# A decoder on one core: first norm's root moved to VectorE, GELUs, result banks and context masks re-ordered

## What is computed

```python
x = layernorm(x + L0_attn(x))              # 16 heads, Student-t kernel on rotated q, k
x = layernorm(x + L0_xattn(x, ctx, ctx))   # mLSTM cell: input and forget gates, 8 heads
x = layernorm(x + L0_ffn(x))               # shared MLP + 8 experts, top 2, GELU
x = layernorm(x + L1_attn(x)); x = layernorm(x + L1_xattn(x, ctx)); x = layernorm(x + L1_ffn(x))

def layernorm(x): return (x - mean(x)) / sqrt(var(x) + 1e-5)

# mLSTM gates
ig, fg = concat(q, k, v) @ igate_w.T + igate_b, concat(q, k, v) @ fgate_w.T + fgate_b
cs = cumsum(log_sigmoid(fg)); log_D = cs[s] - cs[t] + ig[t]; m = max_t(log_D)
# expert e on its tokens: gelu(x @ w1[e] + b1[e]) @ w2[e] + b2[e]
```

## Time and profile before

| what | value |
|---|---|
| median of 3 runs | 2462.15 us (2458.47 to 2462.42) |
| the profiled execution | 2459.75 us |
| its span, first to last instruction | 2457.9 us |
| mean granted TensorE clock | 0.904 of full speed |
| TensorE matmul busy | 1925.9 us (78%) |
| VectorE busy | 1672.9 us (68%) |
| ScalarE busy | 1113.1 us (45%) |
| GpSimd busy | 842.4 us (34%) |
| chain that ended last | TensorE 38%, VectorE 36%, issue 11%, ScalarE 6%, GpSimd 6%, DMA 3% |

### The profile page before, as it was taken

The page is one execution under the profiler, slowest core; times in us unless marked ns, Lnnn a source line. Parts: engine busy times, 40 slices in busy tenths (PEclk is TensorE's granted clock), DMA queues, the critical chain, the costliest instruction groups (busy, mean ns, idle before and its releaser), DMA issues.

```text
span 2457.9 us, 39681 instructions
## 1 busy us (share of the span) xinstructions
PE 1925.9 (78%) x14136; PEld 1375.3 (56%) x14136; DVE 1672.9 (68%) x3985; ACT 1113.1 (45%) x3168; POOL 842.4 (34%) x775
## 2 busy tenths in 40 slices
PE   2786698778886898788886788689877888675698
PEld 1465356645675456645674467545664567553355
DVE  8895794669737893669656993779566973713355
ACT  2462266335642565336642564246533564232234
POOL 0562363226512562317421661236322651211000
PEclk8997799889997999889997999799988999787799
DMA  4000011202030012201030103101120104051000
GB/s 137 1 1 9 13 57 52 77 10 70 1 119 19 16 55 73 64 10 61 6 122 11 56 15 103 34 14 57 50 79 10 69 1 119 9 208 56 9 13 22
DMA packets 72746, 117.08 MB, mean 48 GB/s; under 512 B 7822, under 2 KB 46870, under 8 KB 72038
## 3 DMA queue, kind: packets, MB, share of 16 engines
q1 hardware_dynamic: 67014, 101.42, 12.9%
q0 software_dynamic: 5536, 13.12, 1.8%
HBM read 95.18 MB, written 18.81 MB: 46 GB/s over the span
## 4 chain that ended last, share of the span: by engine, by line
PE 38%; DVE 36%; issue 11%; ACT 6%; POOL 6%; DMA 3%; SPq 1%; DVEq 0%; POOLq 0%; ACTq 0%
PE bank L1355 35%; DVE work L495 11%; DVE bank L504 5%; DVE work L513 3%; DVE work L493 3%; ACT work L952 3%; DVE max L794 2%; POOL hid L1263 2%; PE bank L1359 2%; POOL work L1243 1%; ACT act_row L952 1%; DMA hid<-y_sorted,slot_id 1%; POOL work L1238 1%; DVE acc L712 1%; DMA w_ring<-in_w_routed 1%
## 5 line engine op out<-in xcount | busy, mean ns | idle before, releaser
L1355 PEld LDWEIGHTS bank<-work 128*128 128x128 f32 (+2 forms) x5152 | 387.8, 200 | 182.7 <-issue 181.5
L1355 PE MATMUL bank<-work 128*128 128x128 f32 (+2 forms) x5152 | 418.8, 307 | 69.2 <-DVE max L794 42.2
L952 ACT ACTIVATE work<-bank 128x512 f32<-128x512 f32 (+1 forms) x560 | 247.0, 516 | 311.9 <-PE bank L1355 256.6
L495 DVE TENSOR_TENSOR work<-bank,table_space 64x512 f32<-64x512 f32 x512 | 352.2, 688 | 6.8
L1231 POOL TENSOR_TENSOR work<-work 128x512 f32<-128x512 f32 x128 | 163.3, 1276 | 350.5 <-DVE work L495 248.7
L952 ACT ACTIVATE work<-work 128x512 f32<-128x512 f32 (+1 forms) x338 | 196.7, 618 | 169.8 <-DVE work L581 73.4
L952 ACT ACTIVATE work<-work,negmax 128x128 f32<-128x128 f32 x512 | 199.0, 390 | 100.2 <-DVE negmax L515 100.2
L1238 POOL TENSOR_TENSOR work<-sb_ident,nrm 128x512 f32<-128x512 f32 x128 | 133.1, 1039 | 274.4 <-ACT nrm L952 274.4
L1355 PE MATMUL bank<-work,table_space 128*128 128x512 f32 x256 | 141.3, 634 | 89.9 <-DVE negmax L515 59.4
L952 ACT ACTIVATE hid<-bank,w_ring 128x128 f32<-128x128 f32 x480 | 136.5, 370 | 160.0 <-PE bank L1355 159.9
L493 DVE TENSOR_TENSOR work<-bank,table_space 128x512 f32<-128x512 f32 x256 | 173.8, 679 | 32.4 <-POOL work L1243 20.0
(11 more groups left out here) (287 smaller groups left out, 3414.8 us busy)
## 6 DMA issues: line engine op xcount, KB each, us to landing
w_ring<-in_w_routed SPq DMA_DIRECT2D x120, 514.0 KB, 4.3
x_quad<-x_sorted SPq DMA_DIRECT2D x24, 256.0 KB, 2.9
y_sorted<-y_quad SPq DMA_DIRECT2D x24, 256.0 KB, 2.7
x_T<-in_x_T POOLq DMA_DIRECT2D x9, 256.0 KB, 3.1
x_row<-in_x_row POOLq DMA_DIRECT2D x9, 256.0 KB, 3.9
ctx_T<-in_ctx_T SPq DMA_DIRECT2D x8, 256.0 KB, 2.6
work<-in_ctx_row SPq DMA_DIRECT2D x8, 256.0 KB, 3.0
out<-act_row SPq DMA_DIRECT2D x8, 256.0 KB, 2.3
```

The source lines that it names most:

```text
L495: last = v.tensor_tensor(rows(wk[i + 1][o]), rows(src[p]), sinT[o, s].unsqueeze(1).broadcast_to([DH0, GB, N]), ALU.mult)
L952: return nc.scalar.activation(o, i, f, **k)
L1355: return nc.tensor.matmul(o, l, r, start=start, stop=stop, skip_group_check=True)
```

## The change

1. Norm: the first norm's 1/sqrt is no longer made by ScalarE. VectorE makes it itself (`inverse_root`): half the variance, a starting value from the bits, three Newton steps, 11 instructions on `[128, 4]`. It stands between the copies of blocks 2 and 3.
2. GELUs: those of units 7 and 8 run before the gates' Exp and Ln, so the table is changed behind unit 8 and not behind unit 6. TensorE's transpose of `row_x`, the gates' matmul and the two gate transposes move behind units 7, 8, 10 and 14 (before: 6, 7, 9 and 11).
3. VectorE's gate steps are cut into more pieces and spread between the copies.
4. Banks: the down results of blocks 4, 6, 8, ... go to bank 7, the others to bank 6; a down waits for the copy of the block two before it, and block 4 for `attn_out`.
5. Masks: GpSimd starts the masked contexts behind `gate_max` and not behind `attn_out`.

The diff:

```diff
--- before.py
+++ after.py
@@ -144,6 +144,7 @@
         norm_x, norm_t = Norm("norm_x"), Norm("norm_t")
         centre, centred = sb("centre", 128, GB), sem("centred")
 
+        half_var, root = sb("half_var", 128, GB), sb("root", 128, GB)
         nrm = sb("nrm", 128, 2, 8)
         norm_rows = sb("norm_rows", 128, 2, N)
         negmax = sb("negmax", 128, 2, GB)
@@ -230,6 +231,10 @@
 
             return min(GB, BLOCKS - GB * q)
 
+        def y_bank(i):
+
+            return 7 if i > 3 and i % 2 == 0 else 6
+
         def prob_T_bank(h):
 
             return 6 if h < H0 - 5 else (h - (H0 - 5)) % 2
@@ -453,6 +458,19 @@
 
                 norm_stats(n, src)
                 norm_apply(n, g, i, src, dst, per, ahead)
+
+            def inverse_root(n):
+
+                half, y, y2 = half_var[:], n.rstd[:], root[:]
+                link(v.tensor_scalar(half, n.mv[:, :, 1], 0.5, 0.5e-5, ALU.mult, ALU.add))
+                link(v.tensor_scalar(y.bitcast(i32), half.bitcast(i32), -0.5, 1593268703.0, ALU.mult, ALU.add))
+                for step in range(3):
+                    link(v.tensor_tensor(y2, y, y, ALU.mult))
+                    link(v.scalar_tensor_tensor(y2, y2, -1.0, half, ALU.mult, ALU.mult))
+                    last = v.scalar_tensor_tensor(y, y2, 1.5, y, ALU.add, ALU.mult)
+                    if step < 2:
+                        link(last)
+                last.then_inc(n.ready, 1)
 
             def bc(m):
 
@@ -551,6 +569,8 @@
                     c = slice(b * N, b * N + N)
                     last = v.tensor_tensor_scan(m_g[:, c], one_row, a_g[:, c], -3.0e38, ALU.mult, ALU.max)
                 link(last)
+
+            def gates_parts(g, d):
 
                 link(v.tensor_copy(m_parts[0:8, :], m_g[:]))
                 link(v.tensor_tensor(logf[:], m_g[:], m_parts[0:8, :], ALU.subtract))
@@ -701,7 +721,7 @@
                 q = i // GB
                 if q >= 2 and i % GB == 0:
                     dve.wait_ge(y_stored[q % 2], g * (LOAD // 2 * 16) + q // 2 * 16)
-                v.tensor_copy(y_quad[q % 2][:, i % GB], rows(bank[6])[:, i % GB]).then_inc(y_out, 1)
+                v.tensor_copy(y_quad[q % 2][:, i % GB], rows(bank[y_bank(i)])[:, i % GB]).then_inc(y_out, 1)
 
             def combine(g):
 
@@ -741,6 +761,10 @@
                     norm_stats(norm_x, resid_a)
                 if experts:
                     take_block(2, g)
+                if heads:
+                    dve.wait_ge(norm_x.stats, tally(g, d, LNS, 1))
+                    inverse_root(norm_x)
+                if experts:
                     take_block(3, g)
                 if heads:
                     norm_apply(norm_x, g, 0, resid_a, row_x, ahead=d)
@@ -748,20 +772,28 @@
                     take_block(4, g)
                 if heads:
                     gates_forget(g, d)
-                    gates_scan(g, d)
                 if experts:
                     take_block(5, g)
                     take_rows(2, g)
                     take_block(6, g)
                 if heads:
+                    gates_scan(g, d)
+                if experts:
+                    take_block(7, g)
+                if heads:
                     gates_max(g, d)
+                if experts:
+                    take_block(8, g)
+                if heads:
+                    gates_parts(g, d)
+                if experts:
+                    take_block(9, g)
+                    take_rows(3, g)
+                    take_block(10, g)
+                if heads:
                     gates_columns(g, d)
                 if experts:
-                    take_block(7, g)
-                    take_block(8, g)
-                    take_block(9, g)
-                    take_rows(3, g)
-                    for i in range(10, BLOCKS):
+                    for i in range(11, BLOCKS):
                         take_block(i, g)
 
             def experts_norm(g):
@@ -1046,9 +1078,8 @@
                 for n in range(SLOTS):
                     fn(k2[n], bank[1][:], ACT.Copy, scale=slot_mask[:, n:n + 1]).then_inc(k2_masked, 1)
 
-            def attn0_norm(g, d):
-
-                norm(norm_x, g, 0, ahead=d)
+            def attn0_T(g, d):
+
                 act.wait_ge(stored, tally(g, d, 32, -16) if d else 16)
                 act.wait_ge(x_tr, tally(g, d, 2, 1))
                 fn(seq_T[:], bank[1][:], ACT.Copy).then_inc(x_T_sb, 1)
@@ -1113,12 +1144,17 @@
                         attn0_slot(s, g, d)
                     if experts:
                         for j in IN_SLOT[s - DRAIN]:
-                            gelus(j, g, heads and j == 6)
+                            gelus(j, g)
+                if experts:
+                    gelus(7, g)
                 if heads:
-                    attn0_norm(g, d)
+                    attn0_T(g, d)
+                if experts:
+                    gelus(8, g, heads)
+                if heads:
                     gates_forget(g, d)
                 if experts:
-                    for j in range(7, UNITS):
+                    for j in range(9, UNITS):
                         gelus(j, g, j == UNITS - 1)
                 if heads:
                     gates_total(g, d)
@@ -1266,7 +1302,7 @@
             def xattn(g, d):
 
                 pool.wait_ge(in_ctx, tally(g, d, 32, 32))
-                pool.wait_ge(attn_out, tally(g, d, 1, 1))
+                pool.wait_ge(gate_max, tally(g, d, 1, 1))
                 for h in range(H1):
                     if d and 2 <= h < 4:
                         pool.wait_ge(quad_tr, g * LOAD + h + 1)
@@ -1481,11 +1517,13 @@
                 i = j - 2
                 if i == 0:
                     pe.wait_ge(moe_acc, g + 1)
+                elif i == 4 and heads:
+                    pe.wait_ge(attn_out, tally(g, d, 1, 1))
                 else:
-                    pe.wait_ge(y_out, g * BLOCKS + i)
+                    pe.wait_ge(y_out, g * BLOCKS + (i if i < 4 else i - 1))
                 for c in range(CH):
                     pe.wait_ge(gelu, g * GELUS + CH + i * CH + c + 1)
-                    last = mm(rows(bank[6])[:, i % GB], rows(hid[i % 4])[:, c],
+                    last = mm(rows(bank[y_bank(i)])[:, i % GB], rows(hid[i % 4])[:, c],
                               w_ring[i % RING][:, I0 + c * N:I0 + c * N + N], start=c == 0, stop=c == CH - 1)
                 last.then_inc(half_down, 1)
 
@@ -1564,20 +1602,21 @@
                     if s >= DRAIN:
                         for j in IN_SLOT[s - DRAIN]:
                             unit(j)
+                unit(7)
                 if heads:
                     attn0_T(g, d)
-                unit(7)
+                unit(8)
                 if heads:
                     gates_of_tokens(g, d)
-                for j in (8, 9):
+                for j in (9, 10):
                     unit(j)
                 if heads:
                     gate_a_columns(g, d)
-                for j in (10, 11):
+                for j in (11, 12, 13, 14):
                     unit(j)
                 if heads:
                     gate_tot_columns(g, d)
-                for j in range(12, UNITS + 1):
+                for j in range(15, UNITS + 1):
                     unit(j)
 
             gw = res["gate_w"]
```

## The result

| | before | changed |
|---|---|---|
| median, runs beside one another | 2460.31 us (2457.71 to 2462.42, 4 runs) | 2403.39 us (2400.74 to 2406.48, 4 runs) |
| ratio, 95% interval | | 0.977 (0.9759 to 0.9782) |
| profiled execution, span | 2459.75, 2457.9 us | 2406.48, 2404.7 us |
| mean granted clock | 0.904 | 0.900 |

The change takes 2.3% off, 57 us. The forecast was 2393 us: the measured time is inside the range and ten microseconds above the forecast. The span is 53.2 us shorter; the sum had said 69.

The account below looks back on a forecast made before the run. TensorE's path from the down of unit 6 to the last down sets the end, with waits for VectorE and ScalarE. Gains 67.2 + 1.6 + 0.4 = 69 us off 2459.75: 2390.6, median 2.4 above, 2393; range 2385 to 2416.

Parts of the forecast that it names:

- the sum: Whole program: 67.2 us from seven rounds, 1.6 from the heads-alone round, 0.4 from the last: 69 us off 2459.75.
- the stretch: TensorE from the down of unit 6 to the start of the last down, 36.29 us before; forecast gain 9.6 a round.
- Stops: TensorE's new stops in the stretch: 0.7 at row_x, 0.7 third copy, 1.3 GELU, 0.3 and 0.3: 3.3 us.
- 13.5 - 3.8: In the stretch: 13.5 us of old stops, low clock and restarts, against new stops 3.3 and restarts 0.5; given as 9.6.
- 3.3 - 1.6: Heads-alone round: masks no longer hold VectorE's apply, 3.3 us; the root costs 1.6 more; given as 1.6 less, once.
- Neither bound: VectorE's root: 0.20 us an instruction taken; at best 0.17, at worst doubled, 2.2 us more on the path.
- Weights: Rival: weight loads for block 14 come late, at worst 4.8 us in each of seven rounds, 34 us: 2427; chance 0.04.
- L559: Rival: GpSimd's masks get ahead of this VectorE instruction and hold it 3.3 us a round, 23 in all: 2416; chance 0.08.
- The table: ScalarE's table change costs 1.3 us by the rows; by the skill's 2.66, some 10 us less gain.
- the 1.26 us that did no harm: Old TensorE stop ahead of the down of unit 11; the piece behind it took 1.16 us, against 1.06 usual.
- the first rival: A low-clock spell remains around TensorE's new stops, 1.8 us a round, 12.4 in all: 2405; chance 0.12.
- the prediction's own sign of being wrong: Forecast wrong if pieces behind the stops take 1.9, L559 takes over 1 us, or a stop on w_ring's load appears.

Follow-up runs that it names:

- early masks: Changed kernel with part 5 undone, GpSimd's masks again behind attn_out: 2419.66 us, 0.9833 of the kernel before.
- the repeat: The changed kernel run and traced once more, unchanged: 2400.1 us, 0.9753 of the kernel before.
- fillers behind the combine: Idle products in TensorE's 8.0 us stop: 56 on gates first 2408.12 us, on changed kernel 2427.76; three more stops filled, 2451.02; 28 on gates first, 2379.58.
- gates first: Changed kernel with the gates' matmul moved ahead of the down of unit 8: 2384.73 us, 0.9684 of the kernel before.
- fillers: Changed kernel with four idle identity products ahead of the down of block 7, in the 1.11 us stop: 2402.1 us, 0.9759 of the kernel before.
- one bank: Changed kernel with part 4 undone, all down results in bank 6: 2413.91 us, 0.9806 of the kernel before.
- root and masks: Kernel before with parts 1 and 5 alone, Newton root on VectorE and later masks: 2448.44 us, 0.9946 of the kernel before.
- banks: Kernel before with part 4 alone, two result banks in turn: 2455.06 us, 0.9968 of the kernel before.
- masks alone: Kernel before with part 5 alone, masks behind the gate maxima: 2457.49 us, 0.998 of the kernel before.

## Why the prediction was right, and where not

**Right: the bound and the arithmetic of the stretch.** In the rounds without a spell, sum to last copy fell by 39.96 - 30.01 = 9.95 us and the stretch by 9.86; forecast 9.6.
- Stops: 3.3 us forecast, 1.8 found (0.20 at row_x for 0.7, 0.49 for the third copy of rows for 0.7, 1.11 at the GELU for 1.3, none for 0.3 and 0.3). The rest of the new stretch, pieces and restarts, was 23.3 us in the sum and is 26.43 - 1.8 = 24.6. The two errors, 1.5 and 1.3 us, nearly cancel. That the sum is right within 0.3 us is in part luck.
- Two slips of 0.1 us in the sum: 13.5 - 3.8 is 9.7, not 9.6, and 3.3 - 1.6 is 1.7, not 1.6. They move the forecast by under 1 us.
- The root took 11 instructions at 0.20 us, with the bits as cheap as the rest (0.17 for the int32 instruction). Neither bound was needed.
- Banks, in the changed kernel, 1.4 us of an undisturbed stretch: the stops for a copy did go.
- Weights: landing 3.4, 4.6 and 12.0 us (minimum, median, maximum) against the earlier trace rows, and TensorE waited for one once in the program, as before. The rival is out.
- L559, now L579, is not held: 0.68 us. That rival is out, and it is GpSimd that pays, 2.46 for 2.04, which is hidden.
- The table: the next GELU starts 1.30 us after the load began (1743.28 to 1744.58), as in rows 3. The Trainium skill (ScalarE: Activation LUTs, What ACT_TABLE_LOAD costs) with its 2.66 us would have put that GELU 1.4 us later. This trace does not agree with it; the row decides.
- The masks belong to the root: shown by the run with early masks. The instruction held is a tensor_scalar on 128 x 4 numbers with one input, 2.19 us against 0.16, and by the records it began 0.08 us ahead of the mask that held it. The Trainium skill (SBUF - State Buffer, SBUF: two separate sides) has an exclusive lock between GpSimd and VectorE instructions that read two SBUF inputs or run in a two-port mode, held for a whole instruction. Whether this instruction runs in such a mode no run shows. The trace agrees with the lock, and does not bear out that the first to start keeps it, unless the records are off by that 0.08 us.

**Wrong: one step.** "I expect no low clock because each new stop is at or under the 1.26 us that did no harm." The stop at the GELU was 1.11 us, and behind it the clock fell to 1.2 GHz in four of seven rounds of one trace and two of seven of the other, at 3.1 us each. That is the first rival, which had a chance of 0.12, at 1.8 us in every round, 12.4 in all. It was right about the cause and wrong about the size in a round: that 4 x 3.1 gives the same 12.4 is chance. Its 2405 is nearer to the measured time than the forecast's 2393. By the prediction's own sign of being wrong, pieces of 1.9 us behind the stops, the forecast failed in those rounds. The length of a stop is no criterion: the same 1.11 us did harm in one round and none in the next, and with early masks stops of 2.2 and 1.1 us in one stretch did none in seven rounds.

The second half of the miss was in no rival. I assumed that a stage which the change does not touch keeps its time. Of eight rounds in the two traces with an undisturbed stretch and a round behind them, seven lost 2.6 us behind tok, again by clock. Without low clock the seven stretches would have gained 7 x 9.95 = 69.7 us (67.2 in the sum), and the round with heads alone gave 4.2 in this trace and 2.8 in the repeat (1.6 in the sum). The clock took back 4 x 3.1 = 12.4 in the stretches and 5.9 behind tok, and a late store 2.2.

**What stays open.** Which of the two places is hit in a given round. The two complement each other: of 12 full rounds in two traces of the changed kernel, the period was 262.5 to 263.3 in eleven and 259.73 in one. All kernels of the study show the same grouping; this is a count of the periods (from the second on) in ten traces of nine kernels, those with fillers behind the combine left out:

| period, us | where |
|---|---|
| 259.4 to 259.8 | gates first 5, changed 1, fillers 1 |
| 262.5 to 263.4 | changed 11, masks early 5, fillers 2, one bank 2 |
| 264.0 to 264.7 | one bank 2 |
| 265.3 to 266.7 | fillers 3, one bank 2, masks early 1, gates first 1, root and masks 1 |
| 267.7 to 267.9 | banks 2 |
| 269.4 to 270.0 | before 5, root and masks 5, banks 3, masks alone 4 |
| 271.6 to 272.8 | before 1, masks alone 2, banks 1 |

Most periods stand in a few groups, and a small gain in the stretch either leaves a round in its group or moves it to the next: of the 3.0 us of root and masks 0.3 came in most rounds, of the banks' 2.2 nothing in half of them, while the 0.7 us of gates first came with some 2.4 more a round. This is a count; no run shows what makes the groups. Why a stop's place in time matters so much was not tried. The Trainium skill (TensorE: Matmul & The Clock Gate, Part 1) says that the chip watches TensorE's activity in a rhythm that runs by itself and does not start with the kernel. That two executions of one program had their spells in different rounds agrees with it; no run here shows the rhythm.

Also unexplained is why one or two stores of the last results land in 3.9 to 4.1 us and not 2.1 (the combine is then some 2 us later; once in this trace, twice in those of gates first and of the fillers, not at all in the repeat).

## What to carry to other kernels

Where an engine's clock follows its activity, work out the path first, and then count each remaining stop twice: an edit that removes stops gains what it says only in the rounds in which no spell of low clock follows, and a spell may return in a stage that was not edited. Do not judge a stop by its length alone: one of 1.1 us was followed by low clock in some rounds, and stops of 2.2 and 1.1 us, placed otherwise, in none. Moving one piece, which shortened and shifted the stops, took 15 us off; filling the stop took off nothing. Each was tried once, so try more than one order and read every round of each trace. Before filling or speeding an idle engine, look whether its next piece waits for another engine; low clock beside VectorE's chain was free here.

## What the runs showed of the hardware that I had not expected

- A stop of 1.11 us was followed by 1.2 GHz pieces in some rounds and full-speed ones in others of the same program (1.89 against 1.17 us for the same down), and by another choice of rounds in the next execution. With early masks stops of 2.2 and 1.1 us in one stretch left the granted clock at 1.00 in seven of seven rounds.
- With the same work behind the stop at the row maxima, one round had the full clock back three pieces earlier than the other: the same scores took 1.17 us in one and 2.09 in the other.
- A VectorE instruction of 0.16 us on 128 x 4 numbers was held for two masks of GpSimd in a row (2.19 us), not for one.
- 56 fp32 products of 128 x 128 took 14.38 us at the full clock, 0.257 us each, as 112 instructions.
